# Moving the small scatters and the rotary sum inside GpSimd's step order of an attention stage

## The reference, cut to what matters

```python
def xattn(q, kv, seg_id, ...):             # 16 heads of 128, rotary part of 64 per head
    kv_c, q_c = kv @ W_kvc, q @ W_dq
    q_nope, q_rope = heads(q_c @ W_uq), rope(heads(q_c @ W_qr))
    k_nope, v, k_rope = heads(kv_c @ W_uk), heads(kv_c @ W_uv), rope(kv_c @ W_kr)
    scores = (q_nope . k_nope + q_rope . k_rope) * scale, masked by seg_id
    return (softmax(scores) . v) @ W_o

def moe(h):                                # 16 experts, 6 chosen for each token
    scores = softmax(h @ gate_w.T)
    topk_w, topk_idx = top_k(scores, 6)
    return sum over the 6 of topk_w * (silu(h @ w_gate[e].T) * (h @ w_up[e].T)) @ w_down[e].T

x = x + xattn(layernorm(x), ctx, ...)
x = x + moe(layernorm(x))
```

## Time and profile before

| | |
|---|---|
| median of 3 runs | 2090.32 us (2089.49 to 2098.65) |
| the profiled execution | 2089.45 us, its span 2087.7 us |
| PE busy in the span | 1836.0 us (88%) |
| DVE, ACT, POOL busy | 1205.9, 870.9, 822.2 us |
| mean granted TensorE clock | 0.943 of full speed |
| attention steps | first L871 at 178.78 us, the last at 677.76 us |

### The profile page before, as it was taken

The page is one execution under the profiler, slowest core; times in us unless marked ns, Lnnn a source line. Parts: engine busy times, 40 slices in busy tenths (PEclk is TensorE's granted clock), DMA queues, the critical chain, the costliest instruction groups (busy, mean ns, idle before and its releaser), DMA issues.

```text
span 2087.7 us, 39748 instructions
## 1 busy us (share of the span) xinstructions
PE 1836.0 (88%) x13025; PEld 1086.0 (52%) x13029; DVE 1205.9 (58%) x2650; ACT 870.9 (42%) x1790; POOL 822.2 (39%) x691
## 2 busy tenths in 40 slices
PE   1586998998989489999999999997569989999998
PEld 1335666666655256666666666664444434444443
DVE  7854777777766433333333333332785677777776
ACT  3435877777666134334444344442232222212211
POOL 3102336555565533444344444442001344554542
PEclk7698999999999789999999999999689999999999
DMA  5314557776765256666676676453210345565554
GB/s 195 111 61 125 165 177 170 176 181 186 157 148 127 54 168 163 142 141 163 142 166 142 145 170 124 94 87 60 92 45 12 114 143 186 169 210 202 189 181 164
DMA packets 149136, 294.82 MB, mean 141 GB/s; under 512 B 40432, under 2 KB 77936, under 8 KB 144688
## 3 DMA queue, kind: packets, MB, share of 16 engines
q1 hardware_dynamic: 97968, 157.48, 26.5%
q0 software_dynamic: 46368, 126.29, 24.8%
q10 hardware_dynamic: 4608, 8.52, 1.3%
HBM read 426.00 MB, written 78.33 MB: 242 GB/s over the span
## 4 chain that ended last, share of the span: by engine, by line
PE 66%; issue 8%; POOL 8%; DVE 8%; ACT 5%; DMA 4%; another core or an unknown queue 1%; ACTq 0%; SPq 0%; POOLq 0%; DVEq 0%
PE bank L205 19%; PE bank L207 19%; PE bank L206 19%; POOL expert_tokens L2114 3%; PE bank L999 2%; DMA x_sum<-x,work_arena 2%; DVE work_arena L1466 2%; PE bank L1026 2%; ACT xt_arena L1246 1%; POOL work_arena L2091 1%; DVE work_arena L168 1%; DVE ln_st L155 1%; POOL xt_arena L2100 1%; DMA x<-token_rows,work_arena 1%; POOL xt_arena L2110 1%
## 5 line engine op out<-in xcount | busy, mean ns | idle before, releaser
L205 PE MATMUL bank<-work_arena,xt_arena 128*128 (+1 forms) x1285 | 417.9, 327 | 6.9 <-DVE xt_arena L174 3.3
L206 PE MATMUL bank<-work_arena,xt_arena 128*128 (+1 forms) x1285 | 417.7, 327 | 0.0
L207 PE MATMUL bank<-work_arena,xt_arena 128*128 (+1 forms) x1285 | 417.7, 327 | 0.0
L2187 POOL DMA_INDIRECT x_sum<-x,work_arena x111 | 176.3, 1589 | 400.3 <-DMA x_sum<-x,work_arena 176.7
L205 PE MATMUL bank<-work_arena 128*128 128x512 f16 (+1 forms) x680 | 260.7, 386 | 48.5 <-DVE work_arena L1466 20.0
L1940 DVE TENSOR_TENSOR xt_arena<-xt_arena,bank 128x352 f32<-128x352 f32 x111 | 57.8, 521 | 372.4 <-PE bank L207 347.7
L206 PE MATMUL bank<-work_arena 128*128 128x512 f16 (+1 forms) x680 | 261.1, 386 | 0.0
L207 PE MATMUL bank<-work_arena 128*128 128x512 f16 (+1 forms) x680 | 260.4, 385 | 0.0
L205 PE MATMUL bank<-xt_arena,work_arena 128*128 128x512 f16 (+1 forms) x560 | 212.7, 380 | 1.0 <-DVE xt_arena L174 1.0
L206 PE MATMUL bank<-xt_arena,work_arena 128*128 128x512 f16 (+1 forms) x560 | 212.3, 379 | 0.0
L207 PE MATMUL bank<-xt_arena,work_arena 128*128 128x512 f16 (+1 forms) x560 | 212.2, 379 | 0.0
(11 more groups left out here) (254 smaller groups left out, 3823.1 us busy)
## 6 DMA issues: line engine op xcount, KB each, us to landing
work_arena<-expert_w SPq DMA_DIRECT2D x111, 1408.0 KB
work_arena<-expert_w SPq DMA_DIRECT2D x111, 768.0 KB
work_arena<-in_moe_w SPq DMA_DIRECT2D x64, 352.0 KB
expert_w<-work_arena SPq DMA_DIRECT2D x86, 176.0 KB
work_arena<-in_moe_w SPq DMA_DIRECT2D x48, 256.0 KB
work_arena<-in_mlp_w SPq DMA_DIRECT2D x8, 1536.0 KB
work_arena<-in_head_w SPq DMA_DIRECT2D x16, 512.0 KB, 3.5
expert_w<-work_arena SPq DMA_DIRECT2D x64, 128.0 KB
```

Source lines behind the costliest of these rows:

```text
L205: pe.matmul(o, a_hi, b_hi, start=start, stop=False)
L206: pe.matmul(o, a_hi, b_lo, start=False, stop=False)
L207: return pe.matmul(o, a_lo, b_hi, start=False, stop=stop)
L2187: pool.indirect_dma_start(out=xacc[:, :], out_offset=bass.IndirectOffsetOnAxis(ap=rid[:, i:i + 1], axis=0), in_=ysb[:, b % YB, :], in_offs ...
```

## The change

Only GpSimd's stream changes. Three things are done. In step 1 the sum of half 0 goes ahead of `row_low`. In step 2 the low part of half 0 goes ahead of the sum of half 1. The scatters of a batch of two no longer stand four each in steps 3, 0, 1, but three each in steps 3 and 0 of one tile pair and again in steps 3 and 0 of the next (`ready(q) + 4, 5, 8, 9`); the last such batch has them in `ready(q) + 4, 5, 6, 7`, which are the steps 59 to 62.

```diff
+            def places_of(m):
+
+                late = (4, 5, 8, 9)
+                ends = (4, 5, 6, 7)
+                return [(k, q) for q in range(INNER - 2) for k in range(4)
+                        if m == ready(q) + (late if q < INNER - 3 else ends)[k]]
+
...
                 if row_tile(m, 0) is not None:
                     row_rstd(row_tile(m, 0))
+                if t + 1 < NT:
+                    if g in (2, 3):
+                        rope_low_pool(t + 1, g - 2)
+                    if g in (1, 2):
+                        rope_sum_pool(t + 1, g - 1)
                 if row_tile(m, 1) is not None:
                     row_low(row_tile(m, 1))
-                if t + 1 < NT:
-                    if g in (1, 2):
-                        rope_sum_pool(t + 1, g - 1)
-                    if g in (2, 3):
-                        rope_low_pool(t + 1, g - 2)
-                for k in range(3):
-                    if m - 4 - k in SCORES_AT and BATCHES[SCORES_AT[m - 4 - k]][1] == 2:
-                        place_batch(SCORES_AT[m - 4 - k], 4 * k, 4 * k + 4)
+                for k, q in places_of(m):
+                    place_batch(q, 3 * k, 3 * k + 3)
```

## The result

The changed kernel takes 2081.99 us in the median of 7 runs (2073.74 to 2085.27). The kernel before, timed beside it, takes 2091.99 us (2089.49 to 2100.2). The ratio is 0.9944, with a 95% interval of 0.9923 to 0.9965: faster by 10 us, where 24.7 us were forecast. The stated range ended at 2081 us, so the time lies 1 us outside it. The direction was right and the size was wrong.

A forecast was written before the change was run, and what follows sets the result against it. PE was taken as the bound in undisturbed tiles, with odd tiles losing to waits for POOL's low part. Terms -21.7 - 5 - 1 + 2 + 1 = -24.7 us gave 2065.6 us in the median; range 2057 to 2081 us.

The forecast's parts named there:

- waits at L846 in the odd tiles: PE's turn of rotary queries, tiles 5 to 13: waiting for POOL's low part mostly goes, 21.7 us gained.
- the stall in tile 13: Step 1 of tile 13, PE stalled with "issue" behind eight scatters: expected to vanish, 5 us gained, bounds 0 to 6.4.
- ACT's waits for the sum: ACT waiting 37.5 us for POOL's sum: half of these waits go, PE gains 1 us, bounds 0 to 4.
- end of the stage: Two more scatters between `row_low(13)` and `normalize(62)` make PE's turn 1.3 us late: 2 us lost, bounds 0 to 4.
- even tiles: Three scatters in step 0 may make PE's signals reach others late: 1 us lost, bounds 0 to 14.5.
- The low part of half 0: POOL's step 2: done 22.8 us into the tile, before PE asks at 24.4 to 25.0; reserve 1.6 to 2.2 us.
- A: Half the gain: scatters hold PE's signals, ranks and copies late in ten tiles, or stall moves; 2077.5 us, chance 0.17.
- B: No measurable change: the next tile's scores still wait for ACT's copy until nearly the same moment; 2088 us, chance 0.08.
- C: Slower: signals held in step 3 between turn and copy, 3.6 us in each of ten tiles; 2102 us, chance 0.05.
- signs of a wrong forecast: PE waits above 2 us at L930 or L871 in many tiles, "issue" stalls in steps 0 or 3, longer last steps.

The follow-up runs named there:

- Scatters last: Changed kernel with all scatters of the first seven batches issued behind the loop, after `row_low(14)`; 2165.34 us, ratio 1.0316 to the kernel before.
- order only: Changed kernel with the old scatters, four each in steps 3, 0 and 1, keeping the new order of sums, low parts and `row_low`; 2094.5 us, ratio 1.0047.
- spread: Changed kernel with half 0's sum behind `row_low` in even tiles from 4, and a batch of two's scatters spread over eight steps; 2079.52 us, ratio 0.9917.
- F and G: Two sets of four kernels, each set on one chip beside the kernel before, which took 2096.5 us in F and 2095.18 us in G.
- set E: Four edits of the changed kernel, run on one chip beside the kernel before (2084.37 us); they took 2072.61 to 2094.5 us.
- second pair: Kernel before and changed kernel, both without an edit, profiled again on the chip of set F; 2101.29 us and 2084.53 us.
- scatters only: Changed kernel with the old order of sums, low parts and `row_low`, keeping the new scatter places; 2072.61 us (0.9941) in E, 2084.32 us (0.9944) in G.
- two repeats: Changed kernel without an edit, run again in sets F and G; 2084.53 us (ratio 0.9942) and 2080.05 us (ratio 0.9925).

## Why the prediction was right in direction and wrong in size

By its own terms, with the first pair of profiles (us):

| term | predicted | measured |
|---|---|---|
| waits at L846 in the odd tiles | -21.7 (bounds 16.2 to 23.7) | -17.0 in their steps 3 |
| the stall in tile 13 | -5 (0 to 6.4) | +0.6 in the odd steps 1 |
| ACT's waits for the sum | -1 (0 to 4) | none to be seen; other steps -1.4 |
| end of the stage | +2 (0 to 4) | +1.3 |
| even tiles | +1 (0 to 14.5) | +14.0 in their steps 1 |
| everything else | 0 | +0.5 in tiles 0-3, -5.7 outside the stage |
| sum | -24.7 | -7.7 |

**The low part of half 0** was right as a mechanism. PE no longer waits for L2096 in the tiles 5 to 13, and four of the five odd steps 3 fell from 49.1 to 33.0 us together. The term is 4.7 us short because of tile 5 alone (13.65 us before, 12.76 us after). There PE waits 3.9 us for ACT's L1281 in place of POOL, behind ACT's waits for its weights. The prediction had looked at POOL's 22.8 us against PE's 24.4 us, but not at what else the turn waits for; ACT's DMA waits (11.3 us in the profile before) were not in the sum.

**The even tiles** are the step that failed. It was priced at 1 us "a run of three ends before the scores of step 1 are done", with bounds up to 14.5 us, and measured 14.0 us. Only the signals were considered. The sum of half 0 was placed in step 1 of tile 6 by asking what it makes of POOL and of the low part, and the possible collision was named and then covered by the low part's reserve of 1.6 to 2.2 us. But it was VectorE that was held, and it is VectorE's split on which PE's ranks wait. That chain has no reserve: the earlier trace rows has its five waits already, so that each microsecond on the split is one on PE. The rule was right, and it was charged to the wrong chain. Scatters last isolates 5.4 us of it; order only shows that it needs no moved scatters; the three kernels with the sum behind `row_low` show that it goes with the sum's place. Of the 14.0 us, 6.0 are the ranks' longer wait, nearly all of it this collision; 3.5 are stalls with "issue" behind the three scatters of step 0, which the prediction had put at next to nothing because these scatters end before the scores of step 1 are done; and 4.4 are mostly the lower clock. Why the clock falls in some of these steps and not in others with the same wait stays open. Nor does it need a collision to get there: spread has 62.6 us without one, by waits behind late loads.

**The stall in tile 13** was expected to go, because it fell behind a run of eight scatters. It did not: with no scatter in step 1, PE stands still in the same chain of matmuls, a line earlier than in the earlier trace rows:

```profile
595.23 0.22 PE L857 MATMUL bank<-work_arena 128*128 128x128 f16 x1 [1.88 <-issue]
597.33 0.26 PE L858 MATMUL bank<-work_arena 128*128 128x128 f16 x1 [1.89 <-issue]
```

The step is 14.21 us long before and 14.12 us after, 12.8 to 15.2 us in the runs of F and G that have it, and 7.20 us in all four kernels of set E, in spread, and 7.21 us in scatters last. So it is absent where there are no scatters, but three scatters in step 0 suffice for it, and the old order on chip E (order only) doesn't show it with the old places. Why a whole set, and spread on chip G, are free of it stays open. The term of 5 us is thus lost whole, and the prediction's own doubt, that something like it may fall elsewhere, came true as well, in the even steps 1.

**ACT's waits for the sum** went almost wholly (37.5 to 1.5 us), more than the half that was forecast, and PE got nothing of it. Its own wait for ACT's copy rose from 13.6 to 18.4 us. In this pair ACT's waits for loads rose by 14.9 us beside it; in the second pair its waits for the sum fell as much (30.5 to 1.5 us) and those for loads rose by 2.9 us, so that where ACT's time went isn't shown.

**The end of the stage** came out at +1.3 us for the tail in place of 2 us, but as a sum of larger things. The turn that needs `normalize(62)` started 0.06 us behind its end at 678.32, after a wait of 3.75 us:

```profile
678.38 1.11 PE L887 MATMUL bank<-id,xt_arena 128*128 128x128 f32 x4 [3.75 <-issue]
```

That is 3.1 us later behind the scores of step 63 than before, where 1.3 us were forecast. The steps 60 to 62 were 3.4 us shorter (17.5 against 20.9 us), which the prediction didn't have; in them PE's wait for `row_low` at L912 fell from 3.0 to 1.3 us. What comes behind was 1.6 us longer. So the mechanism was right, its size too small, and the term fits by luck.

**Luck in the total.** Of the 7.7 us between the two spans, 5.7 lie in stages whose program is the same. The terms of which the prediction speaks come to -2.0 us in this pair, and to about -8.6 of -13.8 us in the pair of set F. That the median lies only 1 us outside the range is no sign that the sum was nearly right. The range's lower end also doesn't follow from its words: all terms at their good ends but ACT's give 31.1 us and 2059 us, not 2057.

**The rivals.** A came nearest, with 2077.5 us; the median is 2081.99 us, and 2080.05 and 2084.53 us in the two repeats. It named the right place, late ranks in the even tiles, and the right size, half the gain. Its clause "or the stall moves to another place" came true with 3.5 us. It had the cause only in part: the collision is not in it, and the moved scatters alone cost little (scatters only). B and C did not come about: in the tiles 7 to 13 the next tile's scores waited only 1.1 to 1.4 us, mostly for ACT's copy, and step 3 of the even tiles, where C had its hold, took 8.17 us in the tiles 4 to 12 as in tile 8 before. The signs of a wrong forecast that the prediction named (a wait above 2 us at L930) appeared in three tiles, 6, 8 and 10.

## What to carry to other kernels

When work is moved on GpSimd, look at what VectorE does at that moment, and at who waits for VectorE, before looking at GpSimd's own reserve: a sum of 1.3 to 1.4 us held VectorE for 0.9 to 1.1 us in two different places, both on a chain with no slack. Two disturbances that each cost a microsecond should not be priced apart when both end in one wait. And once the latest releaser of a wait is removed, list the others with their times, the loads behind an in-order engine included.

## What the runs showed of the hardware that was not expected

- A VectorE operation of 0.19 us took 1.07 us beside a GpSimd operation, and ended 0.05 us after it. So the small operation lost about as much (0.88 us) as the large one (1.07 us).
- The scatters, whose own transfers are tiny, go with late loads: ACT's waits for weights sum to 0.3 us without scatters in the stage and to 11 to 47 us with them. The loads themselves are the same. They differ that much among kernels with the same scatters too (11.3 us before, 40.0 us in order only), and between two profiles of one kernel (11.3 and 22.8 us before), so how the one delays the other wasn't isolated.
- PE's signals seem to reach other engines late near scatters. VectorE's maxima (L1561) begin with "remote" as the cause of 9.8 us in 5 waits, up to 4.7 us, although the matmuls stand in the trace as finished. Since the trace's ends of matmuls are modelled, a later true end would look the same. Over the stage such waits of all engines sum to 20.1 and 20.8 us in the two profiles before and to 3.4 to 14.3 us in the six with three scatters in each step 0 outside set E. They are absent in scatters last, but also in spread and in all of set E.
- Stalls with "issue" as the cause, inside a chain of matmuls that waits for nobody, occur only with scatters in the stage, and in the same profiles as the "remote" waits, but for 0.2 us in spread. Scatters only has 9.5 us of them on the chip of set G and none on that of set E.
